# Attention and expert layer: the stacked parts of Q and K kept in memory as a ready image and read 96 rows at a time, and another order of the opening

## What is computed

```python
k, q, v = proj(W_key), proj(W_query), proj(W_value)          # (8, 16 heads, 512, 16)
scores = jnp.einsum('bhqd,bhkd->bhqk', q, k) * hd ** (-0.5)
weight = jax.nn.softmax(jnp.where(causal, scores, -jnp.inf), axis=-1)
out = jnp.einsum('bhqk,bhkd->bhqd', weight, v)                # then W_proj
x = layernorm(x + out)
gate_vals, sel_idx = jax.lax.top_k(softmax(x @ router_w.T).T, capacity)   # 129 tokens of 512
h = gelu(x[sel_idx] @ w1 + b1, approximate=False)
x = layernorm(x + scatter_add((h @ w2 + b2) * gate_vals))
```

## Time and profile before

| | |
|---|---|
| median of 3 runs | 968.99 us (968.87 to 969.45) |
| the profiled execution | 969.03 us, span 967.3 us |
| PE busy | 836.3 us, 86% |
| DVE / ACT / POOL busy | 660.6 / 520.5 / 523.2 us |
| opening, to the first `st` matmul | 69.09 us |
| turns 0 to 7 and the end of attention | to about 491 us |
| experts | 491 us to the end |

### The profile page before, as it was taken

How to read it: one execution, slowest core, us unless ns; L and a number is a source line. 1 busy time by engine, 2 the same in 40 slices (tenths; PEclk the granted TensorE clock), 3 DMA queues, 4 the chain that set the end, 5 groups by cost and what they waited for, 6 DMA issues and landing times. The chain is left out here.

```text
span 967.3 us, 17022 instructions
## 1 busy us (share of the span) xinstructions
PE 836.3 (86%) x5864; PEld 627.4 (65%) x5864; DVE 660.6 (68%) x2017; ACT 520.5 (54%) x1010; POOL 523.2 (54%) x622
## 2 busy tenths in 40 slices
PE   4769999999999999977666999998989899898990
PEld 3444454545455454433365989998989899898990
DVE  4467788787878788999759945555474735546464
ACT  2137666666675757544354445564545556454555
POOL 5347565656565653323655256757375645637344
PEclk9769999999999999988878899999999999998996
DMA  4996767687787778201052224325242332422248
GB/s 140 171 172 122 126 125 149 119 144 140 143 144 144 121 143 177 67 2 45 24 200 81 45 42 89 91 40 131 35 125 45 92 64 51 120 34 33 39 125 257
DMA packets 90102, 100.52 MB, mean 104 GB/s; under 512 B 8736, under 2 KB 83488, under 8 KB 89888
## 3 DMA queue, kind: packets, MB, share of 16 engines
q1 hardware_dynamic: 72560, 77.92, 37.6%
q0 software_dynamic: 12800, 16.92, 10.5%
q10 hardware_dynamic: 4656, 4.59, 1.5%
HBM read 65.38 MB, written 33.62 MB: 102 GB/s over the span
## 5 line engine op out<-in xcount | busy, mean ns | idle before, releaser
L510 DVE CUSTOM_DVE_ANT_0 n_ps<-n_ps,tri 128x512 f32<-128x512 f32 (+3 forms) x512 | 238.5, 517 | 75.3 <-PE n_ps L642 73.8
L1080 DVE TENSOR_TENSOR h_lo<-g,h_hi 128x384 fp32r<-128x384 f32 (+1 forms) x184 | 155.2, 851 | 126.3 <-ACT h_hi L1016 126.0
L430 ACT ACTIVATE pt<-st_ps 128x512 f32<-128x512 f32 x320 | 183.9, 601 | 76.0 <-PE st_ps L627 60.9
L1156 PE MATMUL y_ps<-w_parts,h_hi 128*128 128x256 f32 (+1 forms) x1152 | 213.3, 280 | 0.0
L1011 ACT ACTIVATE g<-h_ps,b 128x384 f32<-128x384 f32 (+1 forms) x192 | 104.2, 543 | 197.8 <-PE h_ps L1142 194.9
L1142 PE MATMUL h_ps<-tt_hi,w_parts 128*128 128x384 f32 (+1 forms) x768 | 179.1, 338 | 32.1 <-issue 21.5
L375 POOL TENSOR_SCALAR_AFFINE_SELECT pt<-pt 128x256 f32<-128x256 f32 (+1 forms) x320 | 111.6, 365 | 130.8 <-ACT pt L430 129.8
L1156 PEld LDWEIGHTS y_ps<-w_parts,h_hi 128*128 128x128 f32 (+1 forms) x1152 | 172.4, 178 | 3.3 <-ACT h_hi L1016 0.2
L983 POOL DMA_INDIRECT acc<-y,tok_no x64 | 102.3, 1599 | 120.6 <-DVE y L1094 112.4
L1156 PE MATMUL y_ps<-w_parts,h_lo 128*128 128x256 f32 (+1 forms) x576 | 161.0, 280 | 0.0
L1142 PEld LDWEIGHTS h_ps<-tt_hi,w_parts 128*128 128x128 f32 x768 | 133.6, 200 | 34.4 <-issue 33.2
(11 more groups left out here) (157 smaller groups left out, 1106.1 us busy)
## 6 DMA issues: line engine op xcount, KB each, us to landing
w_parts<-part_d SPq DMA_DIRECT2D x192, 128.0 KB, 6.1
w_raw<-in_w SPq DMA_DIRECT2D x16, 1024.0 KB, 5.6
part_d<-w_raw SPq DMA_DIRECT2D x96, 128.0 KB, 6.1
w_raw<-in_xt SPq DMA_DIRECT2D x8, 512.0 KB, 5.0
res<-in_x SPq DMA_DIRECT2D x8, 512.0 KB, 10.1
x<-res SPq DMA_DIRECT2D x8, 512.0 KB, 7.0
acc<-res SPq DMA_DIRECT2D x8, 512.0 KB, 8.2
fin<-acc SPq DMA_DIRECT2D x4, 512.0 KB, 3.9
```

Of the source, the lines that this page charges most:

```text
L430: nc.scalar.activation(pt[:, slot % PT_RING, n % UP, :], st_ps[at % ST_RING][:, :], ACT.Exp, scale=S_SCALE).then_inc(exp_done, 1)
L510: ins = nc.vector.tensor_tensor_reduce(out=src[:, h, :], in0=src[:, h, :], in1=mask, scale=-1.0, scalar=-BIG_NEG, op0=ALU.add, op1=ALU.min ...
L1080: nc.vector.tensor_tensor(h_lo[:, q % 2, n, 0:cols], g[:, at % G_RING, 0:cols], h_hi[:, q % 2, n, 0:cols].bitcast(F32), ALU.subtract).then ...
L1156: ins = nc.tensor.matmul(y_ps[at % Y_RING][0:rows, 0:C], x[:, q % 2, m, toks], w[e % 2][:, m, :], start=i == 0, stop=i == len(terms) - 1)
```

## The change

The parts are written to memory in another form. `part_d` held each part once. `image_d` holds, for Q and for K of a sequence and half, the 96 stacked rows as they are to stand in `qst` and `kst`, with the eight heads of a row side by side. So a part is written as many times as it stands in a block, once to three times: 6 writes of 128 KB for each tile instead of 3. The read back of a half is then 4 DMAs of 96 rows with 4 KB each, two for each quarter of the heads, instead of 12 DMAs of 16 rows with 8 pieces of 1 KB each. PE waits for each quarter by itself.

The load of `xt` becomes a stage of its own, `xin`. In the main part it stands where `split` stood. The opening is written out by hand: `opening()` replaces turns -3 to -1.

```diff
+OPENING = {
+    5: (("qk", 1, 0),),
+    11: (("qk", 1, 1),),
+    2 * N_QUARTER - 1: (("nmcut", 0, 0), ("nm", 0, 0), ("stack", 1, 0), ("xin", 2, 0), ("qk", 1, 2)),
+    2 * N_QUARTER + 3: (("qk", 1, 3),),
+    2 * N_QUARTER + 6: (("v", 1, 0), ("v", 1, 1), ("v", 1, 2), ("v", 1, 3)),
+}
+def opening():
+    yield "split", 0, 0
+    yield "xin", 1, 0
+    for stage, n in (("qk", 0), ("qk", 1), ("stack", 0), ("centre", 0), ("qk", 2), ("qk", 3)):
+        yield stage, 0, n
+    for n in range(TT):
+        yield "v", 0, n
+    yield "split", 1, 0
+    yield "stack", 0, 1
+    yield "fold", 0, 0
+    for n in range(NAT_LEAD * N_QUARTER):
+        yield "nat", 0, n
+        if n in OPENING:
+            yield from OPENING[n]
+    yield "split", 2, 0
+    yield "xin", 3, 0
 def steps():
-    for i in range(-3, B + 1):
+    yield from opening()
+    for i in range(B + 1):
...
-    part_d = nc.dram_tensor("part_d", [2, 2, 3, 2, P, T], BF16).ap()
+    image_d = nc.dram_tensor("image_d", [2, 2, 2, KQ, HH, T], BF16).ap()
...
                 for part in range(3):
-                    sp.dma_start(part_d[which, b % 2, part, half_, :, :], parts[:, tile % 2, part, :]).then_inc(parts_out[tile % 2], 16)
+                    for at, held in enumerate((Q_PARTS, K_PARTS)[which]):
+                        if held == part:
+                            to = image_d[which, b % 2, half_, at * D:(at + 1) * D, :, :].rearrange("d h n -> h d n")
+                            sp.dma_start(to, parts[:, tile % 2, part, :]).then_inc(parts_out[tile % 2], 16)
...
-                for which, stack, blocks in ((0, qst, Q_PARTS), (1, kst, K_PARTS)):
-                    for at, part in enumerate(blocks):
-                        src = part_d[which, b % 2, part, n, :, :].rearrange("(h d) n -> d h n", d=D)
-                        sp.dma_start(stack[at * D:(at + 1) * D, b % 2, HH * n:HH * (n + 1), :], src).then_inc(stack_in[n][b % 2], 16)
+                for quarter in (2 * n, 2 * n + 1):
+                    heads = slice(4 * (quarter % 2), 4 * (quarter % 2) + 4)
+                    for which, stack in ((0, qst), (1, kst)):
+                        sp.dma_start(stack[0:KQ, b % 2, 4 * quarter:4 * quarter + 4, :],
+                                     image_d[which, b % 2, n, :, heads, :]).then_inc(stack_in[quarter][b % 2], 16)
...
-                if n % (NU // 2) == 0:
-                    pe.wait_ge(stack_in[n // (NU // 2)][b % 2], 16 * BLOCKS * (b // 2 + 1))
+                if n % N_QUARTER == 0:
+                    pe.wait_ge(stack_in[n // N_QUARTER][b % 2], 32 * (b // 2 + 1))
```

More of the change, by code:

```diff
@@ L34 @@
 Q_PARTS = (0, 1, 0, 1, 2, 0)
-BLOCKS = len(K_PARTS) + len(Q_PARTS)
+WRITES = len(K_PARTS)
 KQ = len(K_PARTS) * D
@@ L83 @@
     (3, 5, 'split', 3, 0),
+    (3, 5, 'xin', 4, 0),
 )
@@ L93 @@
 ROUND_AT += [(B, place) for place in (1, 5, 12, 16)]
-STARTED = [(-2, stage, n) for stage in ("qk", "v", "stack") for n in range(4)]
-STARTED += [(-1, "stack", 0), (-1, "nmcut", 0), (-1, "nm", 0)]
 AV_PLACES = (4, 5, 6, 7)
@@ L107, in steps @@
             for k in range(10):
-                if (i, g, k) == (-1, 3, 0):
-                    yield "nmcut", 0, 0
-                    yield "nm", 0, 0
                 if 0 <= i < B:
@@ L118, in steps @@
                     yield "av", group, AV_PLACES.index(k)
[L119 to L123, removed]
                 for gg, kk, stage, ahead, n in STAGES:
-                    if (gg, kk) == (g, k) and 0 <= i + ahead < B and (i, stage, n) not in STARTED:
+                    if (gg, kk) == (g, k) and 0 <= i + ahead < B:
                         yield stage, i + ahead, n
-                        if (i, stage, n) == (-1, "qk", 1):
-                            yield "stack", 1, 0
                 place = 10 * g + k
@@ L244, in attention @@
     parts_out = [sem("parts_out0"), sem("parts_out1")]
-    stack_in = [[sem(f"stack{h}{p}") for p in range(2)] for h in range(2)]
+    stack_in = [[sem(f"stack{q}{p}") for p in range(2)] for q in range(4)]
     nat_done = sem("nat_done")
@@ L298, in _ @@
         for stage, b, n in steps():
[L299 to L302, removed]
+            if stage == "xin":
+                sp.wait_ge(x_split, b)
+                load_xt(b)
+                if b == 1:
                     sp.dma_start(wpn[:, :, :], wpn_d.rearrange("(k p) n -> p k n", p=P)).then_inc(wpn_in, 16)
@@ L313, in _ @@
                 if b >= 2:
[L314 removed]
+                    for quarter in (2 * half_, 2 * half_ + 1):
+                        sp.wait_ge(stack_in[quarter][b % 2], 32 * (b // 2))
                 for part in range(3):
[L316 removed]
+                    for at, held in enumerate((Q_PARTS, K_PARTS)[which]):
+                        if held == part:
+                            to = image_d[which, b % 2, half_, at * D:(at + 1) * D, :, :].rearrange("d h n -> h d n")
+                            sp.dma_start(to, parts[:, tile % 2, part, :]).then_inc(parts_out[tile % 2], 16)
             elif stage == "stack":
                 for parity in range(2):
[L320 removed]
+                    sp.wait_ge(parts_out[parity], 16 * WRITES * (2 * b + n + 1))
                 if b >= 2:
                     sp.wait_ge(st_done, ((b - 2) * PAIRS + 4 * (n + 1)) * UP)
[L324 to L327 removed]
+                for quarter in (2 * n, 2 * n + 1):
[3 more added lines that the diff above has]
+                                     image_d[which, b % 2, n, :, heads, :]).then_inc(stack_in[quarter][b % 2], 16)
                 if (b, n) == (B - 1, 1):
@@ L382, in _ @@
                 pool.wait_ge(qk_rest, tile)
-                pool.wait_ge(parts_out[tile % 2], 48 * (tile // 2))
+                pool.wait_ge(parts_out[tile % 2], 16 * WRITES * (tile // 2))
                 link(nc.gpsimd.tensor_tensor(qk_r[:, :], qk_f[:, tile % 2, :], parts[:, tile % 2, 0, :], ALU.subtract))
@@ L453, in _ @@
                     act.wait_ge(qk_rest, tile - 1)
-                    act.wait_ge(parts_out[tile % 2], 48 * (tile // 2))
+                    act.wait_ge(parts_out[tile % 2], 16 * WRITES * (tile // 2))
                 nc.scalar.activation(parts[:, tile % 2, 0, :], ps[:, :], ACT.Copy).then_inc(qk_first, 1)
@@ L519, in _ @@
                 if n >= 2:
-                    dve.wait_ge(parts_out[n % 2], 48 * (n // 2))
+                    dve.wait_ge(parts_out[n % 2], 16 * WRITES * (n // 2))
                 link(nc.vector.tensor_tensor(qk_r[:, :], qk_f[:, n % 2, :], parts[:, n % 2, 0, :], ALU.subtract))
```

## The result

The changed kernel takes **973.71 us** (median of 7 runs, 971.23 to 978.71), the kernel before in the same comparison 968.87 us (7 runs). The ratio is 1.0066, 95% interval 1.0044 to 1.0089: slower by 0.7%, where I had forecast 961.6 us. So I compare places in the opening and the main part, not the ends.

A forecast was written before the change was run, and what follows sets the result against it. PE's own work was taken to bound the main part, and the chain of parts writes and stack reads the opening. Gains of 5.3 and 2.6 us less 0.5 us gave 7.4 us off 969.03 us: 961.6 us, range 956 to 967 us.

The forecast's parts named there:

- The moved load: Opening: `xt` of sequence 2, behind three stack reads and six tiles on SP, lands at 62.7 us and costs 0.5 us.
- w: Opening: transfer time of a tile's six writes (768 KB), taken as 4.0 us at half the fast rate, 195 GB/s.
- r: Opening: time to read a half stack (1.5 MB), taken as 4.5 us, with 5.8 us from issue to landing.
- the rival: Opening: late `xt` load gates the exps, 971.9 us with w = 5.9 us; chance 0.08 for slower.
- First natural unit: Opening: PE's first unit of natural scores starts at 32.8 us instead of 35.89, DVE's at 33.4 instead of 36.52.
- Gain at the first `st`: End of the opening: the `st` stream starts at 63.8 us instead of 69.09, a gain of 5.3 us.
- the insertions: Opening: PE's `qk`, `nm` and `v` work between natural units, less DVE's backlog, adds 9.7 us to DVE's time.
- Clock: Behind the first `st`: half of the 5.2 us that PE ran at clock 0.50 goes, a gain of 2.6 us.
- Main part: Turns after the opening: PE's waits stay as before, DMA share falls from 0.75, effect on time 0.
- The rival of full-rate writes: Opening: writes keep the full rate, w = 2.8 us, `xt` is in time, 10.3 us gained, 958.7 us; chance 0.15.

The follow-up runs named there:

- rows8k: The changed kernel with each half stack read by two DMAs of 96 rows of 8 KB instead of four of 4 KB; 973.17 us (one run).
- x_early: The changed kernel with the load of `xt` of sequence 2 moved ahead of the second stack read; 972.08 us, ratio 1.0037 to the kernel before.
- wide_x_early: The changed kernel with Q and K weight columns permuted for one-piece writes and `xt` of sequence 2 loaded ahead of the stacks; 957.01 us, ratio 0.9903.
- wide_writes: The changed kernel with Q and K weight columns permuted on the host, so each write is one piece of 128 rows; 962.08 us, ratio 0.9940.
- narrow_writes: The kernel before with its three writes per tile written down as 8 pieces of 16 rows, same bytes and addresses; 968.87 us, ratio 1.0013.

## Why the prediction was wrong

**The step that failed is "The moved load":** "It lands at 18.6 + 6w + 3 x 5.8 + 2.7 = 62.7 us". The copy that waited for it began at 73.13 us. The error is 10.4 us, and two things make it.
- *A round has terms that I left out.* By my sum a round is 2w + 5.8 = 13.8 us; it took 17.7 and 17.2 us. The sum has the writes at their full rate to the end and the next read right behind them. In fact the writes end unevenly, over 1.8 and 1.0 us, and 0.4 us pass from the last packet to SP's next issue. I had seen 1.6 us of this kind around tile 0, and put them in once at the start, but not ahead of each of the three stack reads. With the late first read (27.84 us, forecast 26.6) this is some 6 us. The Trainium skill ("DMA: Bandwidth & Descriptors", on the anatomy of one DMA) gives, for DMAs issued from GpSimd, about 2 us per DMA that don't scale with its bytes, most of it after the last byte, until a write is confirmed. The trace doesn't agree for these writes from SP: their last packet ends 0.4 us before the next issue, and what stands ahead of it is still moving bytes.
- *r was mis-sized.* Reading a half stack took 6.0 us and more, not 4.5 us: 244 GB/s in place of the 350 GB/s that I took between the ends 133 and 418. The upper end was the best microsecond of a load, whose mean is 345 GB/s even without its start. I also went by the length of the row, and rows8k shows that this isn't what sets the rate. It makes 4.5 us for three reads.

So a round takes 17.4 us on average. My own text had the threshold: the rival decides "from about 3 us more on each stack read". It had the mechanism, the place and nearly the time (971.9 us against 973.71), but only 0.08 of the chance. The nearness of its time is in part luck: it took w = 5.9 us, which wasn't so, and a gain of 2.6 us by the clock, where there was a loss. I weighed it by w alone, and w was the one price that I had right: 1.5 MB in 8.2 us is 4.1 us a tile (forecast 4.0).

What the step cost is read at turn 0. The first `st` is 0.3 us earlier than before. Then PE stands 4.7 us for the exps, where I had 0.5 us for the load. Then the low clock costs 2.4 us more than before (below). By this estimate it is 6.8 us later in all, and 6.85 us were measured. Against my terms (5.3 us gained, 0.5 lost, 2.6 gained) 4.2 us are missed by the load, 5.0 by the clock behind it and 5.0 at the first `st`.

**First natural unit: right in kind, 2.7 us too early.** PE's was at 35.52 us, not 32.8. ACT's tile 3 started at 27.88 (forecast 26.6), `fold` took 1.71 us instead of 1, and then PE waited 0.66 us for the stack, which I had called "not late".

**Gain at the first `st`: 0.3 us instead of 5.3 us.** 2.7 of the missing 5 us come from there. 2.5 us are the wait of the `v` tiles at 63.87 us, behind a tile that waited for its slot. On DVE the pause there is 5.26 us, where I had 2.4 us for the `v` tiles; the other pauses came out 1.0 us below my sum (1.65, 4.08 and 0.54 us for 1.5, 4.8 and 1.0). The 2.4 us didn't even follow from my own numbers, 3.6 us less a backlog of 1.7 to 2.4 us. My account of the insertions had priced PE's work and DVE's backlog, but no wait for a slot; I had written that no wait on `image_d` would exceed 4 us, and two were 6.7 and 7.6 us.

**Clock: the sign was wrong.** I forecast that the 5.2 us at 0.50 behind the first `st` would shrink to half. Instead PE was busy 10.24 us at 0.51 between 72 and 86 us. By an estimate from these numbers that costs 5.0 us against full clock; before, it was 2.6 us. PE had stood from 70 to 74.7 us, waiting for the exps, and the clock was low behind that. In x_early PE stood 3.50 us until 75.46 us and the clock was 0.50 from 74 to 80 us. In wide_x_early, where PE does not stop there, the clock is 1.00 from 60 to 106 us. That much of the term was sound: in a kernel without the gate the low stretch is gone.

**Main part: right.** PE's waits (12.8 us in all, before 13.8) and the length of a turn are unchanged, and the DMA share fell from 0.75 to 0.57, as I had written.

**The rival of full-rate writes was too hopeful as well.** wide_writes took 962.08 us, and my rival "writes at full rate" said 958.7 us. By its sum a round is 2 x 2.8 + 5.8 = 11.4 us and the load of `xt` lands at 18.6 + 6 x 2.8 + 3 x 5.8 + 2.7 = 55.5 us. The rounds took 12.9 us, and the copy that waited for the load began at 60.51 us, 5.0 us late. The same omitted terms stand against it: the writes end at 36.96 and 49.88 us, 0.4 us ahead of the next issue, and the last 1.5 us of them run at 137 GB/s.

One thing stays open: at turn 0 the changed kernel is 6.85 us late, yet the medians differ by only 4.8 us. The profiled execution is 5 us above its own median. 3.7 us of that excess are made behind the opening: it is 7.05 us late in turn 3 and 10.7 us late at the last `x<-res` transfer of the attention half (497.22 against 486.48 us). narrow_writes, whose transfers are those of before, loses 2.4 us in the same stretch of its trace. I have no second profile of the same kernel to say how much of the lateness at turn 0 is particular to this one.

## What to carry to other kernels

Draw a round of dependent transfers with every link: issue to first byte (1.0 us here), bytes at the rate of this form, the uneven end (1.0 to 1.8 us), last byte to the next issue (0.4 us). Such links don't show in the rate of one microsecond from the middle, and they come back in every round. Take a rate from a whole transfer and not from its best microsecond. Where a rival has a threshold, add up all terms that push towards it, not only the one under dispute. And look at the outermost size of a write's target: one piece of 128 rows ran twice as fast here as 8 pieces of 16, and a permutation of weight columns, done ahead of the kernel, was worth some 1.2% here (ratio 1.0066 to 0.9940, 973.71 to 962.08 us) and turned a loss into a gain.

## What the runs showed that I had not expected

- A DMA to few outer rows also takes longer to issue: 0.57 us (median of 192) to 8 outer rows, 0.52 us to 4 outer rows with half the bytes, against 0.43 us for the block writes before and 0.45 us in wide_writes.
- Reads of 96 rows moved 243 to 244 GB/s with rows of 4 KB and 238 to 251 GB/s with rows of 8 KB, over six microseconds: twice as long rows made no difference that can be told.
- The writes of a round don't end together. In the changed kernel the last 1.9 us before 45.2 us ran at 50 GB/s, and the next read had to wait for them.
- A wait of 4.7 us of PE was followed by low clock until 86 us, 0.51 on average from 72 us, although PE was busy for 10.2 of the 14 us. Against full clock that is 5 us by the estimate above, as much as the stall itself.
